# Two PSUM banks for the mixing products at both ends of a strip pipeline, a doubled result tile, and a last store in four pieces

## What is computed

```python
def step1(A, i):  # 1x1, 128 -> 32 channels, writes block i of A; the next i reads it
    Z = _conv(A, w1, 'VALID') + b1
    A = lax.dynamic_update_slice(A, Z, (0, 0, 0, i * EXPAND))
def step2(A, i):  # 3x3, 128 -> 32 channels, the same way
    Z = _conv(A, w2, 'SAME') + b2
    A = lax.dynamic_update_slice(A, Z, (0, 0, 0, i * EXPAND))
def step3(A, i):  # 1x1, 128 -> 1 channel, 128 times
    Z = _conv(A, w3, 'VALID') + b3
    A = lax.dynamic_update_slice(A, Z, (0, 0, 0, i))
A, _ = lax.scan(step1, A, jnp.arange(depth_batch))
A = jax.nn.relu(A)
A, _ = lax.scan(step2, A, jnp.arange(depth_batch))
A = jax.nn.relu(A)
A, _ = lax.scan(step3, A, jnp.arange(CHANNELS))
return A + x
...
x = x + _L2_conv_ref(_gn(x), L2_conv_w1, L2_conv_b1, L2_conv_w2, L2_conv_b2, L2_conv_w3, L2_conv_b3)
x = x + _L3_conv_ref(_gn(x), L3_conv_w1, L3_conv_b1, L3_conv_w2, L3_conv_b2, L3_conv_w3, L3_conv_b3)
```

## Time and profile before

| | us |
|---|---|
| median of 3 runs | 2259.45 (2258.95 to 2266.27) |
| the profiled execution | 2261.95 |
| its span | 2260.2 |
| first product of the pipeline (tile 0, mixing in) | 1266.6 |
| last product of the pipeline (transposes of tile 191) | 2254.1 |

### The profile page before, as it was taken

One profiled execution on the slowest core, in us unless ns is written; L12 is line 12 of the kernel. 1 busy time (PEld: TensorE's weight loads), 2 busy tenths in 40 slices (PEclk: granted clock), 3 DMA queues, 4 the chain that ended last, 5 costly groups with the idle time before them and its releaser, 6 DMA issues. The chain is left out here.

```text
span 2260.2 us, 72910 instructions
## 1 busy us (share of the span) xinstructions
PE 2008.8 (89%) x29714; PEld 1100.8 (49%) x29714; DVE 1636.0 (72%) x3427; ACT 1178.8 (52%) x2577; POOL 1056.9 (47%) x1235
## 2 busy tenths in 40 slices
PE   7798999999999989979995489889999989999996
PEld 5565666566556655645563134333444433333332
DVE  8788888888888888863324778877767655665552
ACT  7677777777777777742222454444444433333330
POOL 0677777777777777749602553332221211111100
PEclk9899999999999999979997689999999999999997
DMA  8011111111111111113446868774444444444434
GB/s 351 20 37 43 45 36 51 36 51 37 51 36 51 37 51 37 50 43 81 101 101 190 294 214 239 218 220 139 129 131 128 132 120 125 127 127 123 118 90 107
DMA packets 225595, 243.79 MB, mean 108 GB/s; under 512 B 125680, under 2 KB 192496, under 8 KB 225264
## 3 DMA queue, kind: packets, MB, share of 16 engines
q1 hardware_dynamic: 225264, 239.13, 35.3%
HBM read 92.48 MB, written 89.65 MB: 81 GB/s over the span
## 5 line engine op out<-in xcount | busy, mean ns | idle before, releaser
L1241 POOL TENSOR_SCALAR l_x<-l_x,l_scale,l_shift 128x384 f32<-128x384 f32 x192 | 150.6, 785 | 595.2 <-PE banks L1655 590.4
L425 POOL TENSOR_TENSOR at_prob<-at_prob,at_inv 128x512 f32<-128x512 f32 x288 | 294.1, 1042 | 117.1 <-DVE at_inv L559 111.8
L1613 PE MATMUL banks<-l_a,l_taps 128*32 128x384 f32 x3456 | 313.3, 493 | 19.1 <-ACT l_r L1313 19.1
L1628 PE MATMUL banks<-l_above,l_taps 128*32 128x384 f32 x1728 | 306.9, 488 | 3.0 <-issue 2.1
L1628 PE MATMUL banks<-l_below,l_taps 128*32 128x384 f32 x1728 | 305.6, 488 | 0.0
L1324 ACT ACTIVATE l_above<-l_below 96x384 f32<-96x384 f32 x144 | 75.5, 524 | 440.4 <-DVE l_below L1499 228.0
L490 ACT ACTIVATE at_prob<-at_prob 128x512 f32<-128x512 f32 x288 | 185.7, 645 | 228.9 <-DVE at_prob L549 228.9
L599 PE MATMUL banks<-at_xn,at_w 128*64 128x256 f32 x2336 | 286.1, 387 | 3.2 <-ACT at_xn L442 3.2
L1485 DVE COPY l_old<-l_a 32x384 f32<-32x384 f32 x576 | 244.2, 424 | 11.4
L641 PE MATMUL banks<-const,at_prob 128*128 128x128 f32 x1152 | 180.6, 284 | 54.4 <-POOL at_prob L425 51.5
L1613 PEld LDWEIGHTS banks<-l_a,l_taps 128*32 128x32 f32 x3456 | 119.5, 110 | 190.3 <-issue 190.3
(11 more groups left out here) (161 smaller groups left out, 3529.8 us busy)
## 6 DMA issues: line engine op xcount, KB each, us to landing
l_x<-both SPq DMA_DIRECT2D x48, 768.0 KB, 4.8
l_rows<-l_r SPq DMA_DIRECT2D x768, 48.0 KB, 2.0
l_work<-both SPq DMA_DIRECT2D x36, 768.0 KB, 6.1
at_k_bd<-at_k SPq DMA_DIRECT2D x584, 32.0 KB, 1.8
load_raw<-in_x SPq DMA_DIRECT2D x36, 512.0 KB, 6.5
both<-l_x SPq DMA_DIRECT2D x24, 768.0 KB, 3.8
out<-l_x SPq DMA_DIRECT2D x24, 768.0 KB, 4.5
both<-x_res SPq DMA_DIRECT2D x20, 768.0 KB, 3.5
```

What stands on the lines that cost most here:

```text
L425: nc.gpsimd.tensor_tensor(prob[i][p][:, :, :], prob[i][p][:, :, :], inv[i][p][:, :].unsqueeze(2).broadcast_to([P, HEADS, WIN]), ALU.mult). ...
L1613: last = nc.tensor.matmul(grid(acc(k)[block_rows(c), :]), e[kind_of(k)][:, dy + 1, dx, :], a[:, k % A_RING, rows_, dx:dx + SIDE], start=(d ...
L1628: last = nc.tensor.matmul(grid(acc(k)[block_rows(c), :]), d[kind_of(k)][:, i, dx, block_rows(c)], of[i][:, groups(k), dx:dx + SIDE], start ...
```

## The change

Nothing is computed differently. Four things move:

- The banks 5 and 6 become `ps_mix`. In the first 26 tiles (`fills`) mixing in takes them in turn and waits only until tile t-2 is copied; in the last 27 (`drains`) mixing out takes them in turn and waits only until tile u-2 is updated. In between each has the bank it had.
- `result` has two places. DVE's update of tile u waits for the transposes of tile u-2 instead of u-1.
- `mix` is cut into `turn_out`, `mix_in` and `mix_out`; in the drain `mix_out(u)` comes ahead of `turn_out`, the transposes of u-1.
- The last strip is stored in four pieces of 192 KB, each when its tile is copied. (A wait of POOL on its own first memset also moves behind six further memsets.)

```diff
-        result = sb("result", [P, TILE])
+        result = sb("result", [P, 2, TILE])
...
-        ps_z, ps_a, ps_f, ps_out = sh.bank[0:Z_BANKS], sh.bank[5][:, 0:TILE], sh.bank[6][:, 0:TILE], sh.bank[7][:, 0:TILE]
+        ps_z, ps_out = sh.bank[0:Z_BANKS], sh.bank[7][:, 0:TILE]
+        ps_mix = [sh.bank[5][:, 0:TILE], sh.bank[6][:, 0:TILE]]
...
+        def fills(t):
+            return t < TURN_LAG + TILE_LEAD - 1
+        def drains(u):
+            return u >= tiles - TURN_LAG - TILE_LEAD
+        def ps_a(t):
+            return ps_mix[t % 2 if fills(t) else 0]
+        def ps_f(u):
+            return ps_mix[(u - tiles + TURN_LAG + TILE_LEAD) % 2 if drains(u) else 1]
+        def result_of(u):
+            return result[:, u % 2, :]
...
-                        sp.wait_ge(s["out_kept"], STRIP_T * (n + 1))
-                        sp.dma_start(out_dram[n * STRIP:(n + 1) * STRIP, :].rearrange("(q p) c -> p q c", p=P),
-                                     x[:, k % X_RING, :].rearrange("p (q c) -> p q c", c=P))\
-                            .then_inc(x_out[k % 2], 16)
+                        runs = STRIP_T if k == strips - 1 else 1
+                        for i in range(runs):
+                            part = slice(i * STRIP // runs, (i + 1) * STRIP // runs)
+                            sp.wait_ge(s["out_kept"], STRIP_T * n + STRIP_T // runs * (i + 1))
+                            sp.dma_start(out_dram[n * STRIP:(n + 1) * STRIP, :][part, :].rearrange("(q p) c -> p q c", p=P),
+                                         x[:, k % X_RING, part].rearrange("p (q c) -> p q c", c=P))\
+                                .then_inc(x_out[k % 2], 16)
...
             nc.gpsimd.memset(a[:], 0.0).then_inc(s["a_zeroed"], 1)
-            pool.wait_ge(s["a_zeroed"], 1)
             for i in range(3):
                 nc.gpsimd.memset(above[i][:], 0.0)
                 nc.gpsimd.memset(below[i][:], 0.0)
             nc.gpsimd.memset(zero[:, :], 0.0).then_inc(s["grids_zeroed"], 1)
+            pool.wait_ge(s["a_zeroed"], 1)
...
-                    wait(dve, s["out_turned"], u - kind_tiles)
-                    nc.vector.tensor_tensor(result[:, :], x_tile(u), ps_f, ALU.add).then_inc(s["updated"], 1)
+                    wait(dve, s["out_turned"], u - kind_tiles - 1)
+                    nc.vector.tensor_tensor(result_of(u), x_tile(u), ps_f(u), ALU.add).then_inc(s["updated"], 1)
...
-                    wait(pe, s["a"], t)
+                    wait(pe, s["a"], t - 1 if fills(t) else t)
...
-                    wait(pe, s["updated"], u)
+                    if u == 0 or drains(u) and not drains(u - 1):
+                        pe.wait_ge(s["a"], TURN_LAG + TILE_LEAD - 1 if u == 0 else tiles)
+                    wait(pe, s["updated"], u - 1 if drains(u) else u)
...
+            def mix(at):
+                u = at - TURN_LAG
+                if drains(u):
+                    mix_out(u)
+                    turn_out(at)
+                else:
+                    turn_out(at)
+                    mix_in(at + TILE_LEAD)
+                    mix_out(u)
```

More of the change, by code:

```diff
@@ L1211, in _ @@
             for i in range(2):
-                sp.wait_ge(x_out[i], 16 * (strips // 2))
+                sp.wait_ge(x_out[i], 16 * (strips // 2 + (STRIP_T - 1 if i == (strips - 1) % 2 else 0)))
         @block.gpsimd
@@ L1299, in keep_a @@
                     act.wait_ge(old_kept[2], k - A_RING + 1)
-                nc.scalar.activation(a[:, k % A_RING, 1 + at:1 + at + TR, inner], grid(ps_a), ACT.Relu,
+                nc.scalar.activation(a[:, k % A_RING, 1 + at:1 + at + TR, inner], grid(ps_a(t)), ACT.Relu,
                                      bias=bias1[:, image(k)]).then_inc(s["a"], 1)
@@ L1465, in update @@
                     xt = x_tile(u)
-                    nc.vector.tensor_tensor(xt, xt, ps_f, ALU.add).then_inc(s["updated"], 1)
+                    nc.vector.tensor_tensor(xt, xt, ps_f(u), ALU.add).then_inc(s["updated"], 1)
                     dve.wait_ge(s["updated"], u + 1)
@@ L1631, in fold, with turn_out @@
                 last.then_inc(conv[i], 1)
-            def mix(at):
+            def turn_out(at):
                 u = at - TURN_LAG - 1
@@ L1641, in mix, with mix_in @@
                     for q in range(TILE // P):
-                        last = nc.tensor.transpose(ps_out[:, q * P:(q + 1) * P], result[:, q * P:(q + 1) * P],
+                        last = nc.tensor.transpose(ps_out[:, q * P:(q + 1) * P], result_of(u)[:, q * P:(q + 1) * P],
                                                    sh.const[:, C_ID:C_ID + P])
                     last.then_inc(s["out_turned"], 1)
-                t = at + TILE_LEAD
+            def mix_in(t):
                 if has_tile(t):
@@ L1652, in mix, with mix_out @@
                         pe.wait_ge(x_in[n % 3], 16 * (n // 3 + 1))
-                    wait(pe, s["a"], t)
+                    wait(pe, s["a"], t - 1 if fills(t) else t)
                     for c in range(BLOCKS):
-                        last = nc.tensor.matmul(ps_a[block_rows(c), :], m1_b[:, column(k), block_rows(c)], x_tile(t),
+                        last = nc.tensor.matmul(ps_a(t)[block_rows(c), :], m1_b[:, column(k), block_rows(c)], x_tile(t),
                                                 start=True, stop=True)
                     last.then_inc(s["s1"], 1)
-                u = at - TURN_LAG
+            def mix_out(u):
                 if has_tile(u):
@@ L1663, in mix @@
                             pe.wait_ge(rows_in[q][k % 2], 64 * (k // 2 + 1))
-                    wait(pe, s["updated"], u)
+                    if u == 0 or drains(u) and not drains(u - 1):
+                        pe.wait_ge(s["a"], TURN_LAG + TILE_LEAD - 1 if u == 0 else tiles)
+                    wait(pe, s["updated"], u - 1 if drains(u) else u)
                     for c in range(BLOCKS):
-                        last = nc.tensor.matmul(grid(ps_f[block_rows(c), :]), m3[:, kind_of(k), block_rows(c)],
+                        last = nc.tensor.matmul(grid(ps_f(u)[block_rows(c), :]), m3[:, kind_of(k), block_rows(c)],
                                                 rows[:, k % ROWS_RING, i:i + TR, :], start=True, stop=True)
                     last.then_inc(s["f"], 1)
+            def mix(at):
[7 more added lines that the diff above has]
+                    mix_out(u)
             for k in steps:
```

## The result

The changed kernel takes 2250.41 us (median of 5 runs, 2246.05 to 2251.20), the kernel before 2259.45. The ratio of the two over these runs is 0.9947, with a 95% interval of 0.9929 to 0.9966: 0.5% faster, some 12 us by the ratio and 9.0 by these medians. 2243.7 was forecast, with a range of 2238.0 to 2250.5; the measured time lies inside it by 0.1 us only, at its upper edge, and two of the five runs lie beyond it. The measured gain is about 0.6 (by the medians) to 0.8 (by the ratio) of the 15.7 us worked out.

The account below looks back on a forecast made before the run. The prediction took PE's ring of waits for DVE's copies at the end as the bound, with SP nearly as full. Terms 6.7 + 6.4 + 2.0 + 0.6 = 15.7 us off 2259.45 gave 2243.7 us, range 2238 to 2250.5.

Parts of the forecast that it names:

- the forecast case: Whole kernel: 2243.7 us, with the bounds of A to C 2239.5 to 2248; chance 0.62.
- the case of a low clock and folds: Rival for the drain: clock stays low, folds hold products back; B 4.2 and A 4.5, 2248.1 us; chance 0.10.
- B: Last four tiles, product 188 to the end of the last copy: 14.86 us becomes 8.4, gain 6.4 (4.2 to 8.3).
- A: Drain: the last strip's rows come sooner, product 188 starts at 2234.0, not 2240.71; gain 6.7 us (4.5 to 8.7).
- The ring: Drain: product of u, DVE's update, copy of the tile before, transposes, then the next product; 3.55 us per tile.
- The step on SP's waits: Drain, last strips: SP's waits for mixing-out products shrink by 4.4 + 1.0 = 5.4 us.
- the first wait: SP's longest wait in the drain, 5.9 us for product 167, was to shrink by 1.0 us.
- C: Last store: a last piece of 192 KB lands sooner than 768 KB; gain 2.0 us (nothing to 2.7).
- D: Start: two banks bring ACT's copies and a relu sooner; gain 0.6 us, between 0 and 4.2.
- waits only change place: Rival: PE's waits for copies become as many for folds and rows; only C and D left, 2256.9 us; chance 0.08.
- SP is no bound: Rival: SP's moves go faster without waits, PE sets the end; 2229 to 2239, say 2232 us; chance 0.05.
- The slower case: Drain: a store in SP's queue waits for held products and delays the next rows; 2266.3 us or more; chance 0.03.

Follow-up runs that it names:

- block 3 by ACT: Changed kernel with the row moves of block 3 of the last four strips issued by ACT's queue, not SP's: 2242.37 us, ratio 0.9925.
- PE kept busy: Beside block 3 by ACT: that kernel with throwaway products in PE's two pauses at the last group norm, 2239.01 us, ratio 0.9906.

## Why the prediction was right, and where it was off

The mechanism was right, the number only just. The time lies inside the range by 0.1 us, and not among the bounds that the forecast case was given (2239.5 to 2248); it stands where the case of a low clock and folds was put (2246 to 2250.5, 0.10), though B came out between the two cases and A near the forecast. That it fell inside is luck in part.

**The ring and what replaces it: right.** PE's waits for copies go, PE's waits for rows come, SP's moves stand back to back, and product 188 starts behind a landing. Of the signs named for A one didn't come: product 188 starts at 2236.39, not near 2234, and 1.8 us of that are the later arrival at the drain.

**A: 6.1 of 6.7 us in the profiled pair.** The step on SP's waits was sized well: the last row move ends 81.37 us behind the copy of tile 191 before and 76.36 now, 5.0 us sooner where 5.4 was worked out; the first wait shrank by 1.2 (worked out 1.0). Two stores, recorded with 1.01 and 1.62 us where I had 0.58, took 1.5 us of it back. What the step missed is that the profiled drain of before was one with a low clock; in two of the five profiles with the old drain the same ring ran 2.6 us faster, and the gain there is 3.5. One reading was off as well, without touching the sum: the strip behind 2220.16 follows after 14.0 us (2234.16), not 13.3, which is where the store begins.

**B: 5.3 of 6.4.** The mis-sized term is the clock of the last strip: two spacings at the low level were taken, with 2.09 each; there were two of 2.27 and one between the levels, 1.82. For a high clock throughout I had 6.6 us; with block 3 by ACT, with PE kept busy and without, where the clock did stay high in the last strip, it is 7.0. The lower bound had 4.4 us behind the last product's start, where its rows add up to 4.1 (1.51 + 0.56 + 0.56 + 0.87 + 0.56).

**C: 2.0 of 2.0.** In every kernel with the split store the span ends 2.5 to 2.7 us behind the last copy, but for the one with block 3 by ACT alone (3.8), where it was 4.6.

**D: nothing to be seen, 0.6 forecast.** The two can't be told apart by these runs. The reason given for a small gain, that the work units' DMAs set the pace, agrees with the waits: ACT's for DMA grew by 6.9 us, PE's for copies fell by some 7. The 2.7 us that the two profiles differ by at the start are within what executions of any kernel differ there, 283.9 to 288.4.

**The rest.** The forecast subtracted terms of one execution from a median of many. The stretches ahead of the drain differ by some 9 us in the first copy, 4.5 at the start and 3.4 in the last group norm from profile to profile; the pair shown happened to have the group norm spared in the kernel before only. By the ratio the change is worth 12 us (7.7 to 16.0), in which the terms' 13.4, or 10.8 against the drain at the higher clock, both lie.

**The rivals.** That waits only change place is what happened to the start, and to all of the drain without the exchange; PSUM buffers alone gave nothing. This agrees with the sentence quoted from the Trainium skill, "TensorE: Matmul & The Clock Gate", section "HAM oscillation — how this bites in real kernels", for the banks by themselves, and not for banks with the exchange. That SP is no bound fell: sixteen moves without a wait for a product still take 11.4 us, and with a quarter of them gone the drain was 3.0 us shorter; but the bound behind it is close. The Trainium skill, "DMA: Bandwidth & Descriptors", section "Issuing engines are not separate DMA queues", calls the time to initiate a DMA usually small relative to the DMA. Here one move's issue is 0.7 us (11.4 for sixteen) against 2.0 us to its landing, and sixteen in one queue were not small. The slower case didn't come: between the last strips' moves SP has no pause for a store that waits for a product.

## What to carry to other kernels

Here the second buffer opened nothing by itself. It opens a ring only if the order of the engine that closes the ring lets the next product pass the step that waits; look at that order first. When a wait at the end of a pipeline is taken away, read which in-order queue, here that of the DMA issues, is already nearly full behind it, and size the gain by its slack. Take the terms from more than one profile of the kernel before: a stretch that runs at either of two clocks is one reason why a term is right and the difference of medians is not.

## What the runs showed of the hardware that I had not expected

- The same instructions, started within 0.03 us of each other up to just ahead of the same pauses (1.82 and 2.93 us), ran behind them at a granted clock of 1.00 in some executions and of 0.86 in others, which costs up to 3.3 us in one place; the old drain's 65.2 or 67.8 us is a second such place.
- Issuing eight 48 KB DMAs from ACT's queue held ACT for 5.2 to 6.0 us, 0.65 to 0.75 us each, about as long as on SP (7.75 us for twelve, 0.65 each), and the kernel became 3 us longer at its end than with none there.
- A store's issue on SP took 0.58 us in most cases; two between back-to-back row moves are recorded with 1.01 and 1.62 us, though the copies that they need were done. Why is open.
